# Softmax head sums turned into reciprocals on 128 partitions of 32 values, instead of 8 rows of 512

## The reference

```
x = layernorm(x)                               # inner norms left out below
q = xn @ Wq          # 16 heads of 64;   k, v = split(xn @ Wkv)   # one key/value head shared by all
attn = softmax(q k^T / 8, axis=-1)             # 4 batches x 16 heads x 512 x 512
y = layernorm((attn @ v) @ Wo);   x = x + y
router: softmax over 8 experts, the top 2 of each token, weights normed to 1
expert: (up * gelu(gate)) @ down, F = 512;     x = x + weighted sum of two experts
```

## Time and profile before

| | before |
|---|---|
| timed runs, median (lowest to highest) | 622.52 us (621.23 to 623.45) |
| profiled execution, span from first to last instruction | 619.0 us |
| TensorE busy | 576.5 us, 93% |
| VectorE busy | 419.2 us, 68% |
| GpSimd busy | 394.9 us, 64% |
| ScalarE busy | 303.0 us, 49% |
| DMA, share of 16 engines | 12.1% (SP's queue) |

### The profile page before, as it was taken

One profiled execution on the slowest core, in us unless ns is written; L12 is line 12 of the kernel. 1 busy time (PEld: TensorE's weight loads), 2 busy tenths in 40 slices (PEclk: granted clock), 3 DMA queues, 4 the chain that ended last, 5 costly groups with the idle time before them and its releaser, 6 DMA issues. The chain is left out here.

```text
span 619.0 us, 8823 instructions
## 1 busy us (share of the span) xinstructions
PE 576.5 (93%) x2611; PEld 328.8 (53%) x2611; DVE 419.2 (68%) x816; ACT 303.0 (49%) x568; POOL 394.9 (64%) x326
## 2 busy tenths in 40 slices
PE   8899999999999999989999988999998869999980
PEld 6455454454554454445544534444443558888870
DVE  4976659658747978875587789877487468444433
ACT  2345645355555554454656434455636453555530
POOL 5357667658668855698597558859746934454330
PEclk9999999999999999889999999999999999999995
DMA  6111011010101100070000000000006101230005
GB/s 177 69 70 70 25 48 69 1 69 6 65 28 43 71 1 2 4 272 32 2 0 2 1 2 18 18 1 1 9 2 191 46 22 32 66 92 27 26 11 203
DMA packets 23981, 29.29 MB, mean 47 GB/s; under 512 B 4403, under 2 KB 14901, under 8 KB 23936
## 3 DMA queue, kind: packets, MB, share of 16 engines
q1 hardware_dynamic: 21664, 24.50, 12.1%
q0 software_dynamic: 2272, 4.24, 2.0%
HBM read 13.73 MB, written 15.32 MB: 47 GB/s over the span
## 5 line engine op out<-in xcount | busy, mean ns | idle before, releaser
L1095 ACT ACTIVATE prob<-s_ps 128x512 f32<-128x512 f32 x256 | 150.5, 598 | 183.0 <-PE s_ps L1201 181.0
L1019 DVE TENSOR_REDUCE rowmax<-max_ps 128x1 f32<-128x512 f32 x256 | 173.1, 685 | 81.6 <-PE max_ps L1170 79.5
L950 POOL TENSOR_TENSOR fold<-prob 128x1024 f32<-128x1024 f32 x63 | 149.6, 2374 | 95.2 <-ACT prob L1095 94.7
L1215 PE MATMUL pv_ps<-prob,v 128*64 128x512 f32 x512 | 139.1, 623 | 0.0
L1199 PE MATMUL s_ps<-q_hl,khh 128*128 128x512 f32 x256 | 118.0, 461 | 0.6 <-ACT prob L1095 0.6
L1170 PE MATMUL max_ps<-khh,q_hl 128*128 128x512 f32 x256 | 103.6, 410 | 6.5 <-DVE q_hl L1008 3.3
L1201 PE MATMUL s_ps<-q_hm,kly 65*128 65x512 f32 x256 | 102.1, 399 | 0.0
L1199 PEld LDWEIGHTS s_ps<-q_hl,khh 128*128 128x128 f32 x256 | 48.6, 190 | 79.2 <-ACT prob L1095 59.8
L956 POOL TENSOR_TENSOR psums<-fold 128x512 f32<-128x512 f32 x63 | 81.7, 1296 | 4.9
L1170 PEld LDWEIGHTS max_ps<-khh,q_hl 128*128 128x128 f32 x256 | 49.1, 192 | 26.5 <-DVE rowmax L1019 9.4
L1201 PEld LDWEIGHTS s_ps<-q_hm,kly 65*128 65x128 f32 x256 | 48.8, 191 | 9.0 <-issue 3.4
(11 more groups left out here) (227 smaller groups left out, 783.2 us busy)
## 6 DMA issues: line engine op xcount, KB each, us to landing
sorted_rows<-raw_w SPq DMA_DIRECT2D x36, 260.0 KB, 2.6
raw_w<-in_gate_upT SPq DMA_DIRECT2D x8, 512.0 KB, 7.5
wd<-in_downT SPq DMA_DIRECT2D x8, 256.0 KB, 3.6
raw_w<-parts SPq DMA_DIRECT2D x8, 256.0 KB, 4.6
psums<-sorted_rows SPq DMA_DIRECT2D x22, 65.0 KB, 1.8
x<-in_x SPq DMA_DIRECT2D x4, 256.0 KB, 5.8
out<-x SPq DMA_DIRECT2D x4, 256.0 KB, 2.5
xs_first<-sorted_rows SPq DMA_DIRECT2D x15, 65.0 KB, 2.2
```

The lines of the kernel that those rows point to most:

```text
L950: nc.gpsimd.tensor_tensor(fold[:, :, :], prob[:, head % 4, 0:2, :], prob[:, head % 4, 2:4, :], ALU.add).then_inc(prob_folded, 1)
L1019: nc.vector.tensor_reduce(rowmax[:, group % 2, it, i:i + 1], max_ps[:, k % 2, :], AX_X, ALU.max).then_inc(max_done, 1)
L1095: nc.scalar.activation(prob[:, head % 4, jt, :], s_ps[:, k % 2, :], ACT.Exp, scale=SCALE).then_inc(exp_done, 1)
L1215: last = nc.tensor.matmul(pv_ps[DH * hd:DH * hd + DH, :], v[:, b % 2, jt, :], prob[:, head % 4, jt, :], start=(jt == 0), stop=(jt == JT - 1))
```

## The change

Between SUM and NORM the unit's sums take another way:

- SUMS (ScalarE, slot 6) copies `sum_ps`, 128 x 512, into `sums` in SBUF.
- SPREAD (SP, slot 6) reads, with two DMAs, the eight rows that count and writes them as 128 partitions of 32 values (`spread`), 64 partitions each.
- RECIP (VectorE, slot 9) takes the reciprocal of these 128 x 32 values, rounds it to fp32r and subtracts (`halves`).
- GATHER (SP, slot 9) writes high parts and rests back as eight rows of 512 each, into rows 0 to 7 and 32 to 39 of `rhl`, with two DMAs.
- NORM waits for these DMAs and multiplies with 40 rows of `headsel` and `rhl` in place of 128. The rows 8 to 31 are set to zero once.

Around this: `headsel` is loaded by four DMAs behind Wo into a slot of `raw`, zeroed and filled by GpSimd in four steps instead of one; the constant `low_parts` isn't loaded; the semaphores of the row tiles 17 to 38 are shared by two tiles each, so that a tile waits for its pair. In the experts' block SPREAD stands first in SP's list and GATHER behind the first two `wd` loads and one row tile; SUMS stands on ScalarE behind the last RAW.

```diff
-RECIP_AT = (6, 7, 8, 10, 12)
+RECIP_STEPS = ("SUMS", "SPREAD", "RECIP", "GATHER")
+RECIP_AT = (6, 6, 9, 9)
...
-        xs_in = [sem(f"xs_in{k}") for k in range(NT)]
+        xs_in = [sem(f"xs_in{k}") for k in range(FIRST_TILES)] + [sem(f"xs_pair{n}") for n in range((REST + 1) // 2)]
...
         def tail_vector(dve, kind, u, a):
             if kind == "RECIP":
-                quarter = slice(a * P, (a + 1) * P)
-                if a == 0:
-                    dve.wait_ge(sum_mm, 2 * (u + 1))
-                last = nc.vector.reciprocal(rinv[:, quarter], sum_ps[:, quarter])
-                if a == 3:
-                    link(dve, last)
-            if kind == "RSPLIT":
+                dve.wait_ge(spread_in, 32 * (u + 1))
+                link(dve, nc.vector.reciprocal(rinv[:, :], spread[:, :]))
                 if u >= 1:
-                    dve.wait_ge(norm_mm, u * UP)
-                link(dve, nc.vector.tensor_copy(rih[:, :], rinv[:, :]))
-                nc.vector.scalar_tensor_tensor(out=rhl[:, :], in0=rih[:, :].bitcast(F32),
-                                               scalar=low_rows[:, 0:1], in1=rinv[:, :], op0=ALU.mult,
-                                               op1=ALU.add).then_inc(recip_done, 1)
+                    dve.wait_ge(rhl_in, 32 * u)
+                link(dve, nc.vector.tensor_copy(halves[:, 0, :], rinv[:, :]))
+                nc.vector.tensor_tensor(halves[:, 1, :], rinv[:, :], halves[:, 0, :].bitcast(F32),
+                                        ALU.subtract).then_inc(recip_done, 1)
...
+        def tail_sync(sp, kind, u):
+            if kind == "SPREAD":
+                sp.wait_ge(sums_copied, u + 1)
+                if u >= 1:
+                    sp.wait_ge(recip_done, u)
+                for half in range(2):
+                    sp.dma_start(spread[half * P // 2:(half + 1) * P // 2, :],
+                                 sums[half:P:32, :]).then_inc(spread_in, 16)
+            if kind == "GATHER":
+                sp.wait_ge(recip_done, u + 1)
+                if u >= 1:
+                    sp.wait_ge(norm_mm, u * UP)
+                else:
+                    sp.wait_ge(consts_set, 1)
+                for part in range(2):
+                    sp.dma_start(rhl[part * LOW_ROW:part * LOW_ROW + UH, :].bitcast(F32),
+                                 halves[:, part, :].bitcast(F32)).then_inc(rhl_in, 16)
+
         def tail_scalar(act, kind, u, a):
+            if kind == "SUMS":
+                act.wait_ge(sum_mm, 2 * (u + 1))
+                if u >= 1:
+                    act.wait_ge(spread_in, 32 * u)
+                nc.scalar.activation(sums[:, :], sum_ps[:, :], ACT.Copy).then_inc(sums_copied, 1)
...
             if kind == "NORM":
-                pe.wait_ge(recip_done, u + 1)
+                pe.wait_ge(rhl_in, 32 * (u + 1))
...
-                nc.tensor.matmul(sum_ps[:, :], headsel[:, a, :], rhl[:, :], start=True,
+                nc.tensor.matmul(sum_ps[:, :], headsel[0:LOW_ROW + UH, a, :], rhl[0:LOW_ROW + UH, :], start=True,
                                  stop=True).then_inc(norm_mm, 1)
...
-                            pool.wait_ge(consts_in, 96)
-                            nc.gpsimd.tensor_scalar(headsel[:, :, :], hs_raw, 1.0, 1.0, ALU.mult,
-                                                    ALU.mult).then_inc(headsel_set, 1)
+                            link_pool(pool, nc.gpsimd.memset(headsel[:, :, :].bitcast(F32), 0.0))
+                            link_pool(pool, nc.gpsimd.memset(rhl[:, :].bitcast(F32), 0.0))
+                            pool.wait_ge(hs_in, 64)
+                            for part in range(2):
+                                held = slice(part * LOW_ROW, part * LOW_ROW + UH)
+                                nc.gpsimd.tensor_scalar(headsel[held, :, :], hs_raw[held, :, :], 1.0, 1.0, ALU.mult,
+                                                        ALU.mult).then_inc(headsel_set, 1)
+                                pool.wait_ge(headsel_set, part + 1)
...
                 for kind, u, a in steps:
+                    tail_sync(sp, kind, u)
...
+                tail_sync(sp, "SPREAD", last_unit)
                 for k in range(EARLY_ROWS, LIST_TILES[0]):
+                    if k == EARLY_ROWS + 1:
+                        tail_sync(sp, "GATHER", last_unit)
...
-                for quarter in range(4):
-                    tail_vector(dve, "RECIP", last_unit, quarter)
-                tail_vector(dve, "RSPLIT", last_unit, 0)
+                tail_vector(dve, "RECIP", last_unit, 0)
...
                 tail_scalar(act, "RAW", last_unit, UP - 1)
+                tail_scalar(act, "SUMS", last_unit, 0)
...
-                    pe.wait_ge(xs_in[k], 16)
+                    pe.wait_ge(xs_in[tile_in(k)], 16 * tiles_with(k))
```

More of the change, by code:

```diff
@@ L23 @@
 RAW_SLOTS = 5
+SPREAD = 32
+LOW_ROW = 32
 def attention_schedule(units):
@@ L82, in attention_schedule @@
             place(after + SUM_AT[1], 5, "SUM", u, 1)
-            place(after + RECIP_AT[4], 5, "RSPLIT", u, 0)
+            for n, kind in enumerate(RECIP_STEPS):
+                place(after + RECIP_AT[n], 5, kind, u, 0)
             for c in range(UP):
-                place(after + RECIP_AT[c], 5, "RECIP", u, c)
                 place(after + NORM_AT[c], 5, "NORM", u, c)
@@ L111 @@
 OUT_LAG = 5
-RECIP_AT = (6, 7, 8, 10, 12)
+RECIP_STEPS = ("SUMS", "SPREAD", "RECIP", "GATHER")
+RECIP_AT = (6, 6, 9, 9)
 SUM_AT = (-7, 5)
 LAST_SUM_AT = (-7, 4)
-LAST_STEPS = (("RECIP", 0), ("RECIP", 1), ("RECIP", 2), ("RECIP", 3), ("RSPLIT", 0), ("NORM", 0), ("NORM", 1), ("OUT", 0),
+LAST_STEPS = (("SUMS", 0), ("SPREAD", 0), ("RECIP", 0), ("GATHER", 0), ("NORM", 0), ("NORM", 1), ("OUT", 0),
               ("NORM", 2), ("OUT", 1), ("NORM", 3), ("OUT", 2), ("OUT", 3))
@@ L271, in bass_preln_mqa_moe_kernel @@
         headsel = sb(whole, "headsel", [P, UP, P], F32R)
-        rih = sb(whole, "rih", [P, S], F32R)
+        sums = sb(whole, "sums", [P, S])
+        spread = sb(whole, "spread", [P, SPREAD])
+        rinv = sb(whole, "rinv", [P, SPREAD])
+        halves = sb(whole, "halves", [P, 2, SPREAD], F32R)
         rhl = sb(whole, "rhl", [P, S], F32R)
-        low_rows = sb(whole, "low_rows", [P, 1])
         raw = sb(whole, "raw", [P, RAW_SLOTS, S])
         ao = sb(whole, "ao", [P, 2, S])
-        rinv = sb(whole, "rinv", [P, S])
         wof = sb(whole, "wof", [P, PAIRS, P])
@@ L321, in bass_preln_mqa_moe_kernel, with tile_in, tiles_with @@
         down_mm = sem("down_mm")
-        xs_in = [sem(f"xs_in{k}") for k in range(NT)]
+        xs_in = [sem(f"xs_in{k}") for k in range(FIRST_TILES)] + [sem(f"xs_pair{n}") for n in range((REST + 1) // 2)]
+        def tile_in(k):
+            return k if k < FIRST_TILES else FIRST_TILES + (k - FIRST_TILES) // 2
+        def tiles_with(k):
+            return sum(tile_in(n) == tile_in(k) for n in range(NT))
         count = {"dve": 0, "pool": 0, "ln": 0, "ln_pool": 0, "ln_dve": 0}
@@ L685, in bass_preln_mqa_moe_kernel @@
          pv_mm, raw_ready, prob_folded, head_sum, sum_mm, recip_done, norm_mm, ao_ready,
-         out_mm) = [sem(n) for n in names]
+         out_mm, sums_copied, spread_in, rhl_in, hs_in) = [sem(n) for n in names]
         def vector_sums(head):
@@ L783, in bass_preln_mqa_moe_kernel @@
         last_pv = max(n for n, step in enumerate(steps) if step[0] == "PV")
-        tail_steps = [step for step in steps[last_pv:] if step[0] in ("RAW", "RECIP", "RSPLIT", "NORM", "OUT")]
+        tail_steps = [step for step in steps[last_pv:] if step[0] in ("RAW", *RECIP_STEPS, "NORM", "OUT")]
         assert all(step in tail_steps or step[0] in ("PV", "SUM") for step in steps[last_pv:])
@@ L855, in _ @@
                 sp.dma_start(wof[:, :, :], wo.rearrange("(c p) n -> p c n", p=P)).then_inc(wo_in, 16)
+                for half in range(2):
+                    for part in range(2):
+                        row = part * LOW_ROW + half * UH // 2
+                        sp.dma_start(hs_raw[row:row + UH // 2, :, :],
+                                     head_rows[half + 2 * part:P:32, :, :]).then_inc(hs_in, 16)
                 for b in range(1, NB):
@@ L986, in _ @@
                         if b == 0:
-                            dve.wait_ge(consts_in, 96)
+                            dve.wait_ge(consts_in, 64)
                         else:
@@ L1123, in _ @@
                 keep_busy(BUSY["start"])
-                pe.wait_ge(consts_in, 96)
+                pe.wait_ge(consts_in, 64)
                 in_bank = None
```

11 lines of the change are left out of this document (6 added, 5 removed).

## The result

The changed kernel takes 628.05 us (median of 20 runs, 624.96 to 630.74) against 622.28 us for the kernel before in runs beside them (20 runs, 617.94 to 626.67). The ratio is 1.0101, with a 95% interval of 1.0077 to 1.0125: about 6.3 us slower (the two medians are 5.8 us apart). Forecast was 616.0 us (612.0 to 621.5). The profiled execution has a span of 627.4 us, against 619.0.

A forecast was written before the change was run, and what follows sets the result against it. TensorE, busy for 93% of the span, was taken to bound the kernel, with waits at NORM for VectorE's reciprocals. -5.1 - 1.7 + 0.3 = -6.5 us: span 619.0 to 612.5, plus 3.5 gives 616.0 us, range 612.0 to 621.5.

The forecast's parts named there:

- NORM with 40 rows streams the same 512 columns: 0: TensorE's NORM matmul: 40 rows instead of 128 cost no time, as the columns streamed stay the same; 0 us.
- Six waits at NORM, -5.1: TensorE between 100 and 400 us: its six waits at NORM for VectorE's last reciprocal step go, -5.1 us.
- The chain: New path from SUM to NORM: copies, DMAs and reciprocal finish before TensorE comes to NORM, with 2.5 us of slack.
- slow landings: Rival, chance 0.05: the new small DMAs land after 5.0 us, NORM waits 0.9 us in seven units; 625.5 us.
- an engine held by GpSimd: Rival, chance 0.03: VectorE's new cast and subtraction each held 2.7 us by GpSimd, 2.4 us in seven units; 632 us.
- Half-clock episode, -1.7: Behind the fourth unit's 2.10 us wait at NORM: TensorE's stretch at half clock goes with the wait, -1.7 us.
- What is late next is TensorE itself: Once NORM's waits are gone, score, maximum and PV products follow each other on TensorE with no record of a wait.
- nothing on the path: Rival, chance 0.11: the waits are replaced by others of the same length right behind (exponentials, maxima); 622.5 us.
- Start, last unit, paired semaphores: 0, 0, +0.3: Kernel start 0 us; last unit's later DMAs covered by a 3.04 us wait, 0; row tiles waiting for their pair, +0.3 us.
- The 3.5 us between span and runs: Whole kernel: runs lie 3.5 us above the profiled span, so a forecast span of 612.5 us becomes 616.0 us.

The follow-up runs named there:

- both moves: GpSimd's three late sends six slots later, CHOOSE5 two slots later: kernel before 617.21 us, changed kernel 617.87 us, changed kernel with NORM on 128 rows 611.54 us.
- with 128 rows: Changed kernel with NORM's matmul on all 128 rows of headsel and rhl instead of 40: 621.84 us, ratio 0.9965 to the kernel before.
- with 65: Changed kernel with NORM's matmul on 65 rows instead of 40: 622.90 us, ratio 1.000 to the kernel before.
- the late sends: GpSimd's last three row sends of the first router block six slots later, on the changed kernel with NORM on 128 rows: 621.86 us, ratio 0.9966.
- NORM ahead of OUT: Changed kernel, 40-row NORM placed before OUT in the 14 slots that hold both: 625.94 us, ratio 1.0038 to the kernel before.

## Why the prediction was wrong

The step that failed is the sentence "NORM with 40 rows streams the same 512 columns: 0". It is a term of +8.1 us in the attention block. The columns are indeed the same; what I priced was the duration of the instruction, and what costs is the change of shape on both sides of it. The rows were at hand: the kernel before has PV products of 128\*64, and behind them the first score product lasts 0.50 us instead of 0.39 and the next starts 0.34 us later instead of 0.23, and the weight load starts together with its matmul:

```profile
106.54 0.19 PEld L1199 LDWEIGHTS s_ps<-q_hl,khh 128*128 128x128 f32 x1 [0.81 <-ACT prob L1095]
106.54 0.50 PE L1199 MATMUL s_ps<-q_hl,khh 128*128 128x512 f32 x1
...
106.88 0.40 PE L1201 MATMUL s_ps<-q_hm,kly 65*128 65x512 f32 x1
```

I took no distance between starts there.

*Six waits at NORM, -5.1.* Right, in place and size: they are gone, and by the distances between starts they were 5.5 us. The chain was forecast well: reciprocal 0.34 us (0.35 forecast), cast 0.57 and subtraction 0.19 (0.2 each and 0.5 of waiting), RECIP at 95.9 (96.5), NORM never late before the last unit. The two rivals on the new chain, slow landings and an engine held by GpSimd, didn't come about.

*Half-clock episode, -1.7.* Right for that place, wrong for the sum. The one behind the fourth unit's tail went, here and in the kernels with both moves, where this term and the one before it come to 5.7 us by the medians, against 6.8 forecast. But the profile of the changed kernel has 10.2 us more at half clock, in other places. With the 8.1 us of the shape, this and the next point explain why the slower kernel's profile is 8.4 us longer.

*"What is late next is TensorE itself."* Wrong: next were GpSimd's `xl` (1.6 us in the changed kernel, 2.5 with 128 rows) and the maxima. The rival "nothing on the path" had this mechanism, but asked for it right behind NORM; it came 12 us later, in the unit with the largest of the six waits. The profile of before showed GpSimd with no pause over 0.3 us from 259 to 284 us.

*Start, last unit, paired semaphores: 0, 0, +0.3.* About right. The attention block starts 0.5 us earlier; NORM waits 0.96 us for its DMA, covered. The paired tile loads show as a DMA wait in two profiles only, with 128 rows (0.4 us) and with 65 (0.6 us).

*The 3.5 us between span and runs.* They are not all outside of first and last instruction: each run lies 1.7 to 2.1 us above its own span, and the rest is that the profiled execution was quicker than the median. As the same 3.5 us were taken off and put back, the forecast difference doesn't change.

What stays open is when the clock falls. Behind the same pair of waits for q's low part and a maximum (1.55 and 0.49 us) the granted clock between 240 and 260 us was 0.83 in the changed kernel, 0.74 with 128 rows and the late sends, but 1.00 with NORM ahead of OUT and in the kernel before on 40 rows. Two of these windows stand above; here is NORM ahead of OUT, then 128 rows with both moves:

```profile
240.00:260.00 20.00, 17.96 (x74) 8.18 (x74) 16.39 (x37) 9.20 (x18) 11.49 (x12) 1.00 0.01 2
```

```profile
240.00:260.00 20.00, 20.00 (x87) 9.36 (x86) 15.79 (x37) 10.54 (x19) 16.26 (x15) 1.00 0.02 5
```

The same 17.96 us of busy time go with 0.74 in one kernel and with 1.00 in another, so the wait alone doesn't decide it; no run settles what does. Where the waits are gone (last row) TensorE is busy throughout and there is no half clock in the stretch.

## What to carry to other kernels

Cutting the rows of a matmul to what holds data is free only as long as the shape class stays the same: between neighbours of 65 to 128 rows and 128 columns, a matmul on 64 rows costs 0.39 us more than one on 65. Pad with zeros instead, or put matmuls of one shape together. And price a matmul by the distance from the start of its predecessor to the start of the second one behind it, not by its own duration; a weight load that starts only with its matmul marks the place. When a wait goes, follow the engines beside it to the end of their own unbroken stretch: in this kernel the gain ended at GpSimd, which had no pause there.

## What the runs showed of the hardware that was not expected

- A change of shape costs 0.19 to 0.20 us, in a dense stream too; by the count above, 128\*64 to 128\*128 is one as well; it is recorded neither as idleness of the matmuls nor as a longer duration of the small one, but the weight load behind the change starts together with its matmul instead of 0.23 us ahead of it.
- A VectorE operation on 64 columns took 2.18 us beside an addition of GpSimd, while the reciprocals beside it (0.18 us) and from `spread` (319 to 353 ns) never stretched.
- Small DMAs from SBUF to SBUF: in the last unit the second SPREAD issue starts at 475.7 and releases VectorE at 477.49, the second GATHER issue at 479.6 and releases TensorE at 482.14: 1.8 and 2.5 us.
